# Gated attention on one core: two further matmuls of 128 rows by 512 columns into bank 6 behind each score tile of the stretch without weighted products

## The reference, cut to what matters

```python
def _L1_attn_ref(sequence, ln_gamma, ln_beta, Wq, bq, Wk, bk, Wv, bv, Wo, bo, mu):
    ...
    q = _split_heads(x @ Wq.T + bq)      # 16 heads of 8
    k = _split_heads(x @ Wk.T + bk)
    v = _split_heads(x @ Wv.T + bv)
    scale = HEAD_DIM ** 0.5
    scores = jnp.einsum('bhqd,bhkd->bhqk', q, k) / scale
    scores = jax.nn.sigmoid(scores - mu) * jnp.exp(scores)
    scores = scores / jnp.sum(scores, axis=-1, keepdims=True)
    out = jnp.einsum('bhqk,bhkd->bhqd', scores, v)
    ...
    return out @ Wo.T + bo
```

## Time and profile before

| what | value |
|---|---|
| median of 3 runs | 1538.46 us (1536.53 to 1542.48) |
| the profiled execution, own time | 1548.84 us |
| its span, first to last instruction | 1547.0 us |
| mean granted TensorE clock | 0.886 |
| TensorE matmuls busy | 1269.9 us (82%) |
| VectorE busy | 1174.2 us (76%) |
| ScalarE busy | 1118.9 us (72%) |
| gated attention, first to last ScalarE tile | 367.8 to 879.0 us of the span |

### The profile page before, as it was taken

How to read it: one execution, slowest core, us unless ns; L and a number is a source line. 1 busy time by engine, 2 the same in 40 slices (tenths; PEclk the granted TensorE clock), 3 DMA queues, 4 the chain that set the end, 5 groups by cost and what they waited for, 6 DMA issues and landing times.

```text
span 1547.0 us, 22272 instructions
## 1 busy us (share of the span) xinstructions
PE 1269.9 (82%) x8010; PEld 645.8 (42%) x8010; DVE 1174.2 (76%) x2121; ACT 1118.9 (72%) x1584; POOL 278.8 (18%) x377
## 2 busy tenths in 40 slices
PE   6699999986777777777777787788899988788996
PEld 3334444452111111111111145556667766576874
DVE  7878886367697797966669556668978797876898
ACT  4267787658999999999999733455565655967985
POOL 2500002451000000002000034444011035621000
PEclk9589999995788778888788897999999998999998
DMA  5300100004000000100000020013233234001111
GB/s 186 109 23 24 44 24 4 1 11 140 0 21 21 1 21 1 36 21 1 21 1 0 29 116 0 1 25 89 91 99 99 80 103 151 21 28 35 42 48 55
DMA packets 41086, 70.47 MB, mean 46 GB/s; under 512 B 6416, under 2 KB 14864, under 8 KB 40208
## 3 DMA queue, kind: packets, MB, share of 16 engines
q1 hardware_dynamic: 40976, 69.05, 14.5%
HBM read 59.26 MB, written 9.76 MB: 45 GB/s over the span
## 4 chain that ended last, share of the span: by engine, by line
PE 37%; DVE 24%; ACT 20%; issue 13%; POOL 3%; DMA 1%; SPq 1%; DVEq 0%; ACTq 0%; POOLq 0%
ACT SHARED L1134 12%; PE PS L823 5%; DVE SHARED L1170 4%; PE PS L1048 4%; PE PS L1035 3%; PE PS L787 3%; DVE KS L2218 3%; PE PS L645 2%; PE PS L1349 2%; PE PS L712 2%; ACT ROUNDED L2142 2%; PE PS L2036 2%; PE PS L2038 2%; PE PS L2037 1%; PE PS L2045 1%
## 5 line engine op out<-in xcount | busy, mean ns | idle before, releaser
L1134 ACT ACTIVATE SHARED<-PS 128x1536 f32<-128x1536 f32 (+1 forms) x346 | 458.4, 1432 | 34.2 <-PE PS L1035 32.8
L1035 PE MATMUL PS<-QS,KS 48*128 48x512 bf16 (+1 forms) x1006 | 237.2, 461 | 123.4 <-ACT SHARED L1134 118.9
L1170 DVE TENSOR_TENSOR SHARED<-SHARED 128x1536 f32<-128x1536 f32 (+1 forms) x170 | 276.5, 1700 | 45.8 <-ACT SHARED L1134 45.8
L803 ACT ACTIVATE SHARED<-PS 128x512 f32<-128x512 f32 (+3 forms) x384 | 163.8, 493 | 75.4 <-PE PS L791 65.9
L1035 PEld LDWEIGHTS PS<-QS,KS 48*128 48x128 bf16 (+1 forms) x1006 | 40.5, 99 | 365.8 <-ACT SHARED L1134 337.9
L1048 PE MATMUL PS<-SHARED,Vg 128*16 128x512 f32 x1024 | 157.3, 692 | 5.2 <-DVE SHARED L1170 5.1
L2036 PE MATMUL PS<-ROUNDED 128*128 128x512 f32 x328 | 135.8, 414 | 6.2 <-ACT KS L2154 6.2
L732 DVE TENSOR_REDUCE NM<-PS 128x2 f32<-128x1024 f32 (+3 forms) x128 | 124.4, 1019 | 16.0 <-PE PS L718 13.7
L2038 PE MATMUL PS<-ROUNDED 128*128 128x512 f32 x328 | 130.3, 397 | 0.0
L2037 PE MATMUL PS<-ROUNDED 128*128 128x512 f32 x328 | 130.2, 397 | 0.0
L2142 ACT ACTIVATE ROUNDED<-KS 128x512 fp32r<-128x512 f32 x100 | 63.1, 631 | 90.2 <-DVE KS L2218 90.1
(11 more groups left out here) (276 smaller groups left out, 2371.9 us busy)
## 6 DMA issues: line engine op xcount, KB each, us to landing
SHARED<-wx SPq DMA_DIRECT2D x64, 256.0 KB, 3.2
SHARED<-in_moe SPq DMA_DIRECT2D x3, 1600.0 KB, 10.7
SHARED<-wx SPq DMA_DIRECT2D x16, 224.0 KB, 3.0
SHARED<-kx SPq DMA_DIRECT2D x32, 96.0 KB
KS<-kx SPq DMA_DIRECT2D x32, 96.0 KB
SHARED<-wx SPq DMA_DIRECT2D x16, 192.0 KB, 2.9
SHARED<-wx SPq DMA_DIRECT2D x16, 160.0 KB, 2.8
qx<-SHARED SPq DMA_DIRECT2D x16, 128.0 KB, 2.4
```

Source lines behind the costliest of these rows:

```text
L803: act.activation(PB[t % 3][:, h, q0:CH], bank(RING0[n % 3], q0), ACT.Exp, scale=SCORE_SCALE)\
L1035: ins = pe.matmul(bank((v % 2) * GRP + f - a), KS[g % 2][r, h // 2, kt * P:kt * P + P], QS[g % 2][r, h // 2, qh * CH:(qh + 1) * CH], start ...
L1134: act.activation(dst, PS[:, (v % 2) * GRP * CH:((v % 2) * GRP + b - a) * CH], ACT.Exp if second == qh else ACT.Sigmoid, scale=SCORE_SCALE)\
L1170: dve.tensor_tensor(ex_tile(j), ex_tile(j), GR[w % RING][:, 0:(b - a) * CH], ALU.mult)\
```

## The change

A new function issues two matmuls whose stationary operand is the identity (`identb`, 128 x 128, bf16) and whose moving operand is 512 columns of the group's queries (`QS`, 128 rows, bf16). They write bank 6. It is called at positions 20, 21, 0, 1, 2, 3 and 4 of every half, behind the score tile (and at 20 behind `pe_out1`), from pass n = 2 on. Nothing reads what they write: the first weighted product at position 5 starts the sum in bank 6 anew, and the copy of the half before has been made when `pe_out1` runs. That makes 30 calls at positions 20 and 21 and 75 at 0 to 4, 210 matmuls in all.

```diff
+        FILL_AT = (20, 21, 0, 1, 2, 3, 4)
+
+        def pe_keep_clock(pe, g):
+
+            for a in range(2):
+                pe.matmul(bank(6), identb[:, :], QS[g % 2][:, a, 0:CH], start=True, stop=True)
+
         def pe_out1(pe, hf):
...
                         if at == OUT_AT:
                             pe_out1(pe, hf)
+                        if n > 1 and at in FILL_AT:
+                            pe_keep_clock(pe, n // 4)
                     pe_beside_gated(pe, n, j)
```

## The result

The changed kernel is slower: 1549.99 us median (1547.6 to 1556.15, 5 runs) against 1538.46 us of the kernel before (1534.69 to 1542.48, 5 runs). The ratio is 1.0071 with a 95% interval of 1.0048 to 1.0093. The forecast was 1525.9 us. The profiled execution took 1556.15 us with a span of 1554.3 us, 7.3 us more than the one before. Both profiled executions lie above their medians, by 10.4 us before and by 6.2 us after.

What follows compares the result with a forecast made beforehand. ScalarE sets the pace, waiting for TensorE at the low clock. Gains of 3.6 + 6.45 + 4.96 + 1.3 = 16.3 us, less 1.1 and 2.6, give 12.6 us: 1538.46 to 1525.9 us, range 1518 to 1540.

Steps and rivals of the forecast that it cites:

- What bounds the kernel: Gated attention: ScalarE sets the pace and waits for TensorE's score tiles, 31.6 us in 28 waits, 2% of the time.
- The first rival: Behind the table load: the clock holds through the gap in every half, 16.3 to 17.9 us less, about 1521 us; chance 0.20.
- a way to be wrong: Position 20: VectorE's copy comes so late that the turning and the score tiles behind it become the new wait; no size.
- VectorE's chain: Ahead of quotient halves: 26.99 us, already the bound in 3 and 5; in 1, 7 and 13 1.2 us each, 3.6 us.
- The price of a pair at the high clock: Behind score tiles: 0.46 us a pair, bounded by 0.39 and 0.78, hidden under ScalarE's 1.34 us step.
- The gap: ScalarE's table load leaves TensorE 1.7 us of nothing; the clock is lost there in about two of three halves.
- The return of the clock: Behind the gap: pairs at the low level keep TensorE busy without a break, so the clock returns about position 4 to 6.
- the price of 0.4 us: Behind the gap: one tile of 1.85 instead of 1.34 us, less a lead of 0.1; 1.1 us over halves 9 to 12.
- the third rival: Positions 2 to 4: pairs don't bring the clock back, 1.4 us a half on top of today's waits, 1555.5 us; chance 0.12.
- The second fall: Behind positions 9 and 10: the clock falls again in four halves, 1.6 us each in ScalarE's waits; half 9's left standing.
- The quotient halves: Halves 2, 4, 6, 8, 14 at position 5: 1.29 us each, 6.45 us, less 2.6 for 4 of 10 at old cost.

Runs made afterwards that it cites:

- the gap filled: Changed kernel with three more pairs behind position 1 (position 2 in quotient halves), where ScalarE's table load leaves TensorE idle: 1530.87 us, ratio 0.9925 to the kernel before.
- both fills: Changed kernel with three more pairs in the table load's gap and a pair behind positions 9 and 10: 1523.29 us, ratio 0.9883 to the kernel before.
- products' form: Changed kernel with eight matmuls shaped like the weighted products at positions 2, 3 and 4 in place of the pairs: 1532.1 us, ratio 0.9935 to the kernel before.
- the three pairs alone: Changed kernel with its pairs at positions 2, 3 and 4 only: 1550.8 us, ratio 1.0077 to the kernel before.
- a burst of the same matmuls: Kernel before with four pairs, eight matmuls back to back, behind position 2 alone: 1564.68 us, one run.

## Why the prediction was wrong, by its steps

**What bounds the kernel** held. ScalarE sets the pace, and TensorE at the low level costs it 1.24 us a half. The first rival (the clock holds through the gap) said 16.3 to 17.9 us less. With the gap filled 10.9 us came (1530.87 against 1541.72 of the kernel before on that chip), as VectorE's late copy made a new wait at position 20, which the prediction had named as a way to be wrong; with both fills it was 18.4 us (1523.29 against the same). So the gain was there, but the pairs of this change could not reach it.

**VectorE's chain** held: 26.99 us in half 3 with both fills. In the changed kernel it was not the bound: half 3 took 28.83 us (480.71 to 509.54 in its trace), as the second falls had made ScalarE later.

**The price of a pair at the high clock** held: two matmuls last 0.60 us, the work ahead of position 21 was pushed from 410.69 (410.40 and the later start of the trace, 0.29) to 410.89 us and nobody waited. Without positions 2 to 4 the kernel ran as fast as before.

**The gap** was named as the place, and the share of halves was about right: two of three expected, 12 of 15 seen. But it was treated as a property of the gap. The runs with products' form and with two pairs kept the same 1.46 us of idle time and kept the clock in 10 of 15 halves. The reading behind it was short as well: the earlier trace rows end at 785 us, about position 11, and cannot show that the clock stays up through positions 11 to 18.

**The return of the clock is the step that failed, and with it the price of 0.4 us.** I wrote that pairs at the low level keep TensorE busy without a break, so the clock comes back about position 4 to 6, for 0.4 us a half, and that only 4 of 10 quotient halves keep the old cost. The reading behind it was of the earlier trace rows: from 420.40 on TensorE was busy without a break and the clock rose. What was busy there were weighted products and score tiles. The changed kernel was just as gapless from 417.04 on and stayed low until 423.6 us, when the products of position 5 were nearly done: the late end of the span that I named, and the moment at which it had come back before. The price did not fit even that span, since it counted one slow tile where a return at position 6 means three and the products. With the three pairs alone it stayed low through 6.76 us of unbroken work. So half 1, and seven more of the nine ordinary halves much like it, paid for the pairs at 1.93 us a tile (0.37 + 0.48 us) and then still for the products (0.90): 1.75 us where 0.4 were forecast and 1.24 were paid before. That was in part the mechanism of the third rival, given 0.12, though not its reason: the zeros of the identity made no difference, and a burst of the same matmuls did lift the clock. Its sum, 1.4 us on top of 1.24, is what the three pairs alone show (2.68 us); in the changed kernel the clock fell one tile later. That its 1555.5 us lie near 1550 is partly luck, since it had no further second falls in it.

**The second fall** was left standing at four halves. It came in nine, 1.6 us each. This term, put at no change because nothing is added at 9 and 10, failed too. Filling positions 9 and 10 took the changed kernel from 1.0071 to 0.9966 of the one before, 1.05 points, and the kernel before by 0.40 points. The difference of 0.65 is nearly all of the 0.71 that the change lost, though each ratio is only good to about 0.2 points. So the return kept the forecast gain away, and the further second falls made the loss; how the 24 us between forecast and result divide between the two is not measured more closely. Why the fall became regular is only argued: the thin stretch at 9 and 10 loses the clock where the clock has returned early. The traces fit. Read from stretches of 1 us, it was back before the change 10.6 to 10.9 us behind the start of the table load in the four halves with a second fall, and 11.3 to 13.3 us in the five without; in the changed kernel it was back at 10.4 to 10.8 us in eight of the nine. Half 10 never lost it in the gap and had the second fall all the same, and in the run with another stationary operand the second fall also stood behind returns at 11.1 to 11.4 us, so there is no sharp bound. The halves also repeat closely (halves 1, 3, 5 and 7 took 34.05, 33.95, 33.98 and 33.93 us, before 31.8 to 33.4). No run moved the return alone.

**The quotient halves** gained 0.4 us each, not 0.8: waits of 1.87 to 2.66 us became 1.7 to 1.8 in total, as the products ran low in all five of them, where two were expected.

The Trainium skill, page "TensorE: Matmul & The Clock Gate", section "Why this matters for your kernels", says that keeping TensorE busy continuously gets it to the high level. Here a stretch that was 5.00 us busy of 5.00 stood at 0.50 throughout; the measurement decides, and busy time as the trace shows it did not tell whether the clock rises.

## What to carry to other kernels

Filler work that is meant to hold TensorE's clock must be dense enough to hold it or to bring it back, for wherever it runs low it nearly doubles in length in front of the critical engine: one pair a tile cost 0.7%, two pairs at positions 2 to 4 gained 0.9%, one pair a tile plus a filled gap 0.75%. Look for every thin stretch of the loop, not only the largest, since a change in one moved the falls in the next; here filling the gap and the second stretch together gave 1.2%. And when a clock is read from rows as having risen under unbroken work, note which work it was.

## What was not expected of the hardware

A stretch without any idle time can stay at the low level: 6.76 us of score tiles (48 rows in pairs) and single pairs of 128-row matmuls at 0.50, while eight of those 128-row matmuls back to back, 3.19 us, were followed by its rise. The content of the stationary operand made no difference that can be told (1.0057 against 1.0071, with overlapping intervals). The clock fell over a wait of 1.62 us ahead of four small matmuls at the end of a half, and in 10 of 15 halves it did not over a gap of 1.47 us with dense work behind it. In the kernel before it fell in half 1 at 413.2 us, where no idle time of TensorE in the 5 us ahead was over 0.95 us.
